# Lists of the experts' tokens: sums of marks by TensorE in place of scatter and gather through DRAM, masks and marks on GpSimd

## The chip, the cores and the metric

The kernel runs on one core of a Trainium2 chip. The metric is the device time of one execution in microseconds (us). The engines of the core are TensorE (PE in the profile), VectorE (DVE), ScalarE (ACT), GpSimd (POOL) and SyncE (SP), which here only issues DMAs.

## The reference, cut to what matters

One decoder layer on x of 16 sequences x 256 tokens x 256 channels, in float32. It has three parts, each with a residual:

```
x = x + ssm(layernorm(x))                     # a scan over the tokens, 16 states per channel
x = x + align(ctx, layernorm(x))              # DTW: rows of ctx summed where the best path goes
x = x + moe(layernorm(x))                     # 64 experts, the best 2 of each token

logits = x_n @ gate                           # 4096 tokens x 64 experts
weights, selected = top_k(logits, 2);  weights = softmax(weights)
y[t] = sum over i of weights[t, i] * (silu(x_n[t] @ w0[e]) * (x_n[t] @ w1[e])) @ wo[e],  e = selected[t, i]
```

So 8192 entries (token, first or second choice) are to be put into 64 lists, one for each expert, and every expert then works on the rows of its list.

## The kernel before, in words

The stages follow each other as blocks, each with its own instruction streams, and a barrier between them: `states` (the scan), the DTW wave and the trace back, `expand`, `experts`, `combine`.

**`states`** begins with eight loads of x, 512 tokens each (`load_x`, L286). DVE takes the statistics of a group in `mean(p)` (L493), which waits for the semaphore of that one load.

**`expand`** (L1529 on) goes over the 16 sequences b in beats. For each b the work is: ACT makes `apart`, the squared distance of each row to the middle of a token's stretch on the path (`far`, L1929); DVE compares it with `reach` and writes the 0/1 masks `on` (`masks`, L1721, two instructions of 128x256); PE multiplies masks by ctx and adds x (`expanded`, L1984: four matmuls with masks, two with the identity, each of 128x256); ACT copies the sum to x (`added`, L1960, line L1962 in the profile); DVE takes mean and variance and a Newton step; ACT normalizes to `xn` (which SP writes to DRAM); PE transposes it (`turn`), ACT copies it (`take_turned`, L1954), PE forms the logits (`logits`, L2005), DVE finds the eight largest and their places (`largest`, `where`), writes `hot`, the 0/1 marks of the two chosen experts (`mark`, L1782), and their sum `chosen` (`choose`, L1789). PE then counts with two matmuls how many earlier entries an expert has (`rank`, L2015), DVE picks an entry's own place (`pick`, `position`) and `address` (L1815) makes of expert and place a line number `slot`. The beats are skewed: in beat b PE works on `rank(b-3)`, `logits(b-2)`, `expanded(b+1)`, `turn(b-1)`, in this order, and DVE in beat b begins with `masks(b+1)` and later has `statistics(b)`, `largest(b-2)` to `choose(b-2)` and `position(b-3)`, `address(b-3)`.

The lists are made in DRAM: `enter(b)` (L1643) on GpSimd issues, for each tile of 128 tokens and each choice, one indirect DMA that writes 128 numbers of 4 bytes into `bucket` (64 in all). After the last beat, the experts are sorted by their counts (`key`, `above`, `my_rank`, `at_rank`, `order`: short steps to and fro between PE and DVE, L1860 to L1879 and L2036 to L2050), SP loads the weights of the first expert as soon as `order` is there, and GpSimd waits until all 64 scatters have landed and gathers from `bucket` the first 256 entries of each expert in the sorted order (L1684, `entries_i`). PE transposes them to `choice`; DVE makes `table`, the row of x_n for each entry (L1923); GpSimd gathers the rows of the first expert (L1691), and the block ends.

**`experts`** (L2072 on) runs 63 ranks, with a static room for each, and then a loop of late tiles for what is left (one pass here). PE goes by ranks; SP loads the weights of rank k when rank k-4 is done (a ring of 4); GpSimd gathers rows four ranks ahead (`gather`) and scatters the results to `outs` (`scatter`). For a late tile SP reads its entries from `bucket` and loads its expert's weights once PE has signalled that rank 59 is done (`done`, given in rank 60). `combine` adds the two results of each token.

The order of the work is written out by hand: the loops in each engine's block say which step stands before which. In `expand` it is for PE

```
for b in range(B + 3):
    if real(b - 3): rank(b - 3)
    if real(b - 2): logits(b - 2)
    if real(b + 1): expanded(b + 1)
    if real(b - 1): turn(b - 1)
```

and on GpSimd `for b in range(B): enter(b)`.

Of the kernel before, what the change touches and what calls it, by code (L numbers as in the profile page):

```python
# [5 lines left out]
ALU = mybir.AluOpType  # L6
# [8 lines left out]
P = 128  # L15
# [152 lines left out]
def states(K):  # L168
# [7 lines left out]
    with ExitStack() as c:  # L176
# [61 lines left out]
        x_in = [sem(f"x_in{g}") for g in range(NP)]  # L238
# [46 lines left out]
        def _(sp):  # L285

            def load_x(p):
                sp.dma_start(K.x[:, p * PTT:(p + 1) * PTT, :],
                             K.x_dram[p * PT:(p + 1) * PT, :].rearrange("(t p) d -> p t d", p=P)).then_inc(x_in[p], 16)
# [199 lines left out]
        def _(dve):  # L489
# [3 lines left out]
            def mean(p):  # L493
                dve.wait_ge(x_in[p], 16)
# [812 lines left out]
def trace_back(K):  # L1307
# [6 lines left out]
    with ExitStack() as c:  # L1314
# [50 lines left out]
        def _(pool):  # L1365
# [15 lines left out]
            pool.wait_ge(set_up, 10)  # L1381
# [147 lines left out]
def expand(K):  # L1529
# [3 lines left out]
    TABS, COUNTED, RANKED, ORDERED, PLACED, LATE_FROM, LATE_OF, TURNED = range(1, 9)  # L1533
    ENTERED = 2 * TT * 16
    ABOVE, AT_RANK, ORDER, MORE, SERVES, ENTRIES, TABLE = range(1, 8)
    with ExitStack() as c:
# [21 lines left out]
        col, eps, expert, row, ones, earlier = K.col, K.eps, K.expert, K.row, K.ones, K.earlier  # L1558
        picked = ring(2, "ex_picked", [P, 2, 2, E])
        nth = ring(2, "ex_nth", [P, 2, 2])  # L1560
        slot = sb("ex_slot", [P, TT, 2], I32)
# [7 lines left out]
        line = sb("ro_line", [P, 1])  # L1569
# [7 lines left out]
        above = sb("ro_above", [E, E])  # L1577
        my_rank = sb("ro_my_rank", [E, 1])
        at_rank = sb("ro_at_rank", [E, E])
        of_rank = sb("ro_of_rank", [E, E])  # L1580
        lines = sb("ro_lines", [E, 1], I32)
        entries_i = sb("ro_entries_i", [E, 2 * P], I32)
        entries = sb("ro_entries", [E, 2 * P])
# [16 lines left out]
        l_ps = [ps(f"ex_l{u}", [P, 4, P]) for u in range(2)]  # L1600
# [15 lines left out]
        slot_ok, placed = sem("ex_slot_ok"), sem("ex_placed")  # L1616
# [7 lines left out]
        ALL = 12  # L1624
# [15 lines left out]
        def _(pool):  # L1640
            imprecise = dict(allow_small_or_imprecise_dtypes=True)

            def enter(b):  # L1643
                pool.wait_ge(slot_ok, b + 1)
                for t in range(2 * b, 2 * b + 2):
                    for i in range(2):
# [33 lines left out]
            for b in range(B):  # L1680
                enter(b)
# [804 lines left out]
```

## Time and profile before

| | us |
|---|---|
| three runs, median | 1364.31 |
| three runs, lowest and highest | 1362.76, 1365.70 |
| profiled execution, span from the first to the last instruction | 1362.8 |
| of it, first beats of `expand` to the end of its last copy of x (719.3 to 822.0) | 102.7 |
| of it, from there to the first work of `experts` (822.0 to 862.2) | 40.2 |
| of it, `experts` up to the late tile's first product (862.2 to 1307.6) | 445.4 |
| `combine` (1325.0 to 1362.8) | 37.8 |

| engine | busy us | share of the span |
|---|---|---|
| PE | 1039.0 | 76% |
| DVE | 904.0 | 66% |
| POOL | 649.3 | 48% |
| ACT | 574.8 | 42% |

The shortest of the three runs is as long as the span, so next to nothing lies around the span. The shares are averages over stages with different limits; for one stage a timeline shows on which engine each step waits. In a timeline a row is: start, duration, engine, line, operation, result and operands, shape, number of merged instructions, and in brackets the idle time of the engine before it with what ended it. "remote" there means that the semaphore's event came late, by the profile, with no instruction that ended just then.

### The profile page before, as it was taken

The numbers are of one execution on the slowest core, as the hardware profiler recorded it, in microseconds if no ns is written. First come the engines' busy times: TensorE is split into PE (matmuls) and PEld (weight loads), VectorE is DVE, ScalarE is ACT, GpSimd is POOL, SyncE is SP. The second block draws the span as 40 slices with busy tenths as digits, with TensorE's granted clock in tenths as the row PEclk, the third lists the DMA queues.
The fourth block names the chain that finished last, engine by engine and source line by source line (L and its number), as shares of the span: only waits on it lengthen the run. The fifth ranks groups of instructions, "written<-read, shape, count | busy, mean of one in ns | idle before, by whom it ended". The sixth has DMA issues, their size and how long they took to land. (4 is left out here: it accounts for less than half of the span.)

```text
span 1362.8 us, 20764 instructions
## 1 busy us (share of the span) xinstructions
PE 1039.0 (76%) x6769; PEld 921.1 (68%) x6769; DVE 904.0 (66%) x2041; ACT 574.8 (42%) x1282; POOL 649.3 (48%) x591
## 2 busy tenths in 40 slices
PE   4767878778787775776567764699999999999940
PEld 3656767767676774665215653699999888888840
DVE  6999999999999984887986664233232232323218
ACT  3768787787878653443404441121121212111100
POOL 4887888878788832000003555334434344434310
PEclk8999999999999997555778796799999999999985
DMA  8544646465555622123030111788778788888629
GB/s 238 194 137 134 182 146 188 152 186 166 169 172 157 183 59 57 31 43 51 33 123 32 40 40 32 259 275 268 267 259 268 268 274 272 274 271 269 238 75 348
DMA packets 163531, 232.62 MB, mean 171 GB/s; under 512 B 34380, under 2 KB 87996, under 8 KB 162656
## 3 DMA queue, kind: packets, MB, share of 16 engines
q1 hardware_dynamic: 145808, 207.79, 48.7%
q0 software_dynamic: 11280, 19.06, 4.2%
q10 hardware_dynamic: 6336, 4.44, 1.0%
q8 instruction: 55, 0.90, 0.3%
q14 instruction: 52, 0.43, 0.1%
HBM read 203.08 MB, written 23.95 MB: 167 GB/s over the span
## 5 line engine op out<-in xcount | busy, mean ns | idle before, releaser
L1011 PE MATMUL st_y_ps<-ident,st_hc 128*128 128x128 f32 x2048 | 274.0, 292 | 113.9 <-DVE st_hc L530 113.9
L1011 PEld LDWEIGHTS st_y_ps<-ident,st_hc 128*128 128x128 f32 x2048 | 255.5, 203 | 136.5 <-DVE st_hc L530 135.6
L413 POOL TENSOR_TENSOR st_u<-st_dx,codes 128x1024 f32<-128x1024 f32 x127 | 296.5, 2360 | 40.9 <-DVE st_h L522 31.9
L522 DVE TENSOR_TENSOR_SCAN st_h<-st_da,st_u 128x512 f32<-128x512 f32 x256 | 297.7, 1204 | 0.8 <-ACT st_da L749 0.8
L2203 PE MATMUL mo_h<-mo_xt,w 128*128 128x128 f32 (+17 forms) x2048 | 281.1, 288 | 1.9 <-DVE mo_xt L2300 1.9
L2203 PEld LDWEIGHTS mo_h<-mo_xt,w 128*128 128x128 f32 x2048 | 270.4, 192 | 6.7 <-issue 2.7
L2306 DVE TENSOR_TENSOR mo_inter<-mo_silu,mo_h 128x128 f32<-128x128 f32 (+17 forms) x256 | 75.7, 304 | 281.2 <-ACT mo_silu L2277 217.1
L2144 POOL DMA_INDIRECT outs<-mo_o,choice x95 | 93.7, 986 | 232.6 <-DVE mo_o L2317 219.4
L2277 ACT ACTIVATE mo_silu<-mo_h 128x128 f32<-128x128 f32 (+17 forms) x256 | 71.7, 290 | 311.8 <-PE mo_h L2203 210.9
L749 ACT ACTIVATE st_da<-st_delta,st_a_neg 128x510 f32<-128x510 f32 x256 | 171.7, 685 | 57.2 <-DVE st_h L522 52.8
L530 DVE TENSOR_TENSOR st_hc<-st_h,st_cps 128x1024 f32<-128x1024 f32 x128 | 152.7, 1193 | 0.0
L2137 POOL DMA_INDIRECT mo_xg<-xn,table x93 | 90.4, 972 | 34.5 <-issue 28.1
L1295 PE MATMUL wv_e<-wv_r,wv_shift 128*128 128x1 f32 x274 | 75.9, 348 | 40.5 <-DVE wv_r L1233 39.8
L2217 PE MATMUL mo_ot_ps<-mo_inter,wo 128*128 128x190 f32 (+16 forms) x512 | 88.1, 305 | 17.1 <-DVE mo_inter L2306 14.3
L1295 PEld LDWEIGHTS wv_e<-wv_r,wv_shift 128*128 128x128 f32 x274 | 68.5, 312 | 48.1 <-issue 46.1
L756 ACT ACTIVATE st_cps<-codes 128x512 f32<-128x512 f32 x128 | 76.7, 599 | 46.1 <-DVE st_hc L530 41.1
L1647 POOL DMA_INDIRECT bucket<-ex_row,ex_slot x64 | 62.2, 972 | 60.6 <-DVE ex_slot L1817 43.8
L2217 PEld LDWEIGHTS mo_ot_ps<-mo_inter,wo 128*128 128x128 f32 x512 | 73.3, 190 | 24.2 <-DVE mo_inter L2306 19.8
L2209 PE MATMUL mo_o_ps<-wo,mo_inter 128*128 128x256 f32 x256 | 73.9, 392 | 0.0
L1285 ACT ACTIVATE wv_r<-wv_e,wv_edge_big 128x1 f32<-128x1 f32 x137 | 35.8, 261 | 64.6 <-PE wv_e L1295 64.6
L1367 POOL IOTA tb_vacant<- 128x2048 int32 x1 | 1.9, 1867 | 104.9 <-POOLq L1108 104.9
L1233 DVE TENSOR_TENSOR_SCAN wv_r<-wv_m,wv_r,wave 128x64 f32<-128x64 f32 x136 | 47.8, 352 | 4.8
(359 smaller groups left out, 1416.4 us busy)
## 6 DMA issues: line engine op xcount, KB each, us to landing
codes<-bc SPq DMA_DIRECT2D x256, 256.0 KB, 3.8
w<-in_L_ffn_w_dram SPq DMA_DIRECT2D x128, 512.0 KB
wo<-in_L_ffn_wo_dram SPq DMA_DIRECT2D x64, 512.0 KB
co_got<-outs SPq DMA_DIRECT2D x16, 512.0 KB, 6.0
wave<-dist SPq DMA_DIRECT2D x16, 274.0 KB
x<-in_x_dram SPq DMA_DIRECT2D x8, 512.0 KB, 9.2
st_cx<-in_ctx_dram SPq DMA_DIRECT2D x8, 512.0 KB, 4.1
dist<-st_dd SPq DMA_DIRECT2D x32, 128.0 KB, 3.6
```

Of the source, the lines that this page charges most:

```text
L413: nc.gpsimd.tensor_tensor(u_sb[k % URING][:, :, :], dx[p % 2][:, :, :], over_chunks(b_sb[k % BRING]), ALU.mult).then_inc(u_ok, 1)
L522: nc.vector.tensor_tensor_scan(h_sb[k % HRING][:, dh, :], da_ps[dh][:, :], u_sb[k % URING][:, dh, :], 0.0, ALU.mult, ALU.add).then_inc(h_o ...
L530: nc.vector.tensor_tensor(hc_sb[k % RING][:, :, :], h_sb[k % HRING][:, :, :], over_chunks(c_ps[k % 2][:, :]), ALU.mult).then_inc(hc_ok, 1)
L749: nc.scalar.activation(by_batch(da_ps[dh][:, :]), by_batch(delta[p % 2][:, dh, :]), ACT.Exp, scale=a_neg[:, dh, n:n + 1]).then_inc(da_ok, 1)
L756: nc.scalar.activation(c_ps[k % 2][:, :], c_sb[k % CRING], ACT.Copy).then_inc(c_ok, 1)
L1011: m = nc.tensor.matmul(y_ps[t // 2][:, t % 2, dh * P:(dh + 1) * P], hc_sb[k % RING][:, dh, t * P:(t + 1) * P], K.ident[:, :], start=False, ...
L1295: nc.tensor.matmul(e_ps[t % 4][:, 0:1], K.shift[:, :], r[:, t + 1, SW:SW + 1], start=True, stop=True).then_inc(e_mm, 1)
L2137: nc.gpsimd.indirect_dma_start(xg[k % XR][0:n, a, :], None, K.xn_dram[:, :], bass.IndirectOffsetOnAxis(ap=K.table[0:n, at:at + 1], axis=0) ...
L2144: nc.gpsimd.indirect_dma_start(K.outs_dram[:, :], bass.IndirectOffsetOnAxis(ap=K.choice[0:n, at:at + 1], axis=0), o_sb[k % XR][0:n, a, :], ...
L2203: ins = nc.tensor.matmul(h_ps[m][:, i, 0:n], K.w[r][i][:, c_, m * P:(m + 1) * P], xt[u][:, c_, 0:n], start=(c_ == 0), stop=(c_ == DC - 1))
L2217: ins = nc.tensor.matmul(ot_ps[:, c_, 0:n], K.w[r][2][:, m, c_ * P:(c_ + 1) * P], inter[m][:, 0:n], start=(m == 0 and c_ == 0), stop=(m == ...
L2306: nc.vector.tensor_tensor(inter[m][:, 0:n], silu[m][:, 0:n], h_ps[m][:, 1, 0:n], ALU.mult).then_inc(inter_ok, 1)
```

## The change

- The lists are no longer read back from DRAM. For each beat DVE writes `in_list`, four 128x256 marks of an entry's place (`enlist`, in place of `address`), GpSimd writes `valued`, the marks of its expert times its number in the tile and times the tile's number (`value`), and PE adds up `valued` x `in_list` over all 64 (tile, choice) pairs in one bank (`enlisted`): row = expert and part, column = place. After the sort two matmuls with `at_rank` give `choice` at once.
- `masks` goes from DVE to GpSimd.
- The 64 scatters to `bucket` stay, for the late tiles, but are issued in `experts`: one before each rank's gather (two before the first). `slot` is computed once at the end of `expand`. SP waits for all of them (`K.placed`) before the late loop.
- One PSUM bank is freed for the sum: both `l_ps` now lie in one.
- The semaphores of the eight x loads become two: one for the first, one for the seven others; `mean(p)` for p of 1 and more waits for all seven.

```diff
@@ states
-        x_in = [sem(f"x_in{g}") for g in range(NP)]
+        x_in = [sem("x_in_first"), sem("x_in_rest")]
...
-                dve.wait_ge(x_in[p], 16)
+                dve.wait_ge(x_in[min(p, 1)], 16 * (NP - 1) if p else 16)
@@ expand, GpSimd
-            def enter(b):
-                pool.wait_ge(slot_ok, b + 1)
-                for t in range(2 * b, 2 * b + 2):
-                    for i in range(2):
-                        nc.gpsimd.indirect_dma_start(
-                            K.bucket_dram[:, :], bass.IndirectOffsetOnAxis(ap=slot[:, t, i:i + 1], axis=0),
-                            row[:, t, i:i + 1], None).then_inc(placed, 16)
+            def masks(b):
+                u = b % 2
+                pool.wait_ge(apart_ok, b + 1)
+                if b >= 2:
+                    pool.wait_ge(e_mm, b - 1)
+                for h in range(2):
+                    m = nc.gpsimd.tensor_scalar(on[u][:, h, :], apart[u][:, h, :], reach[:, h, b:b + 1], None,
+                                                ALU.is_le)
+                m.then_inc(mask, 1)
+
+            def value(b):
+                pool.wait_ge(hot_ok, b + 1)
+                if b >= 3:
+                    pool.wait_ge(list_mm, b - 2)
...
+                nc.gpsimd.tensor_tensor(by_part[:, :, :, 0, :], hots, in_tile, ALU.mult)
+                nc.gpsimd.tensor_tensor(by_part[:, :, :, 1, :], hots, tile_no, ALU.mult).then_inc(valued_ok, 1)
...
+            pool.wait_ge(reach_ok, 2)
+            masks(0)
+            masks(1)
             routing_constants()
             for b in range(B):
-                enter(b)
-            pool.wait_ge(row_ok, ORDER)
-            pool.wait_ge(placed, ENTERED)
-            nc.gpsimd.indirect_dma_start(entries_i[:, :], None,
-                                         K.bucket_dram.rearrange("(l j) a -> l (j a)", j=2 * P),
-                                         bass.IndirectOffsetOnAxis(ap=lines[:, :], axis=0)).then_inc(placed, 16)
+                if real(b + 2):
+                    masks(b + 2)
+                value(b)
             pool.wait_ge(row_ok, TABLE)
@@ expand, VectorE
-            def address(b):
+            def enlist(b):
                 need(place_at[b])
...
+                if b >= 3:
+                    dve.wait_ge(list_mm, b - 2)
+                for t in range(2):
+                    for i in range(2):
+                        m = nc.vector.tensor_scalar(in_list[b % 3][:, t, i, :], K.place[:, :],
+                                                    nth[:, 2 * b + t, i:i + 1], None, ALU.is_equal)
+                m.then_inc(in_list_ok, 1)
...
-                if real(b + 1):
-                    masks(b + 1)
...
+            nc.vector.tensor_tensor(listed[:, :], bank(list_ps)[:, 0:L], vacant[:, :], ALU.add).then_inc(row_ok, 1)
...
-            dve.wait_ge(placed, ENTERED + 16)
-            nc.vector.tensor_copy(entries[:, :], entries_i[:, :]).then_inc(row_ok, 1)
@@ expand, TensorE
+            def enlisted(b):
+                pe.wait_ge(in_list_ok, b + 1)
+                pe.wait_ge(valued_ok, b + 1)
+                for t in range(2):
+                    for i in range(2):
+                        m = nc.tensor.matmul(bank(list_ps)[:, 0:L],
+                                             valued[b % 3][:, t, i, :, :].rearrange("p a e -> p (a e)"),
+                                             in_list[b % 3][:, t, i, :], start=(b + t + i == 0),
+                                             stop=(b == B - 1 and t + i == 2))
+                m.then_inc(list_mm, 1)
...
                 if real(b - 1):
                     turn(b - 1)
+                if real(b - 4):
+                    enlisted(b - 4)
...
+            for h in range(2):
+                m = nc.tensor.matmul(bank(xt_ps[1])[:, h * E:(h + 1) * E], listed[:, h * P:(h + 1) * P], at_rank[:, :],
+                                     start=True, stop=True)
@@ experts, SyncE and GpSimd
+            sp.wait_ge(K.placed, 2 * TT * 16)
             n = late_count(sp)
...
             for k in range(RANKS):
+                for n in range(k, 2 * TT, RANKS):
+                    enter(n)
                 if k + XR < RANKS:
                     gather(k + XR)
```

Three places where instructions now stand otherwise. The numbers behind a tile's name are its buffers. First GpSimd in `expand`, at its constants and the first sequence's four scatters, before (`ex_slot` is the line number, `ex_row` the entry):

```order
L1674 IOTA ro_at 64x64
L1676 MEMSET late_of 128x66
L1677 MEMSET late_at 128x66
L1647 DMA bucket<-ex_row,ex_slot 278528x1 [waits ex_slot_ok]
L1647 DMA bucket<-ex_row,ex_slot 278528x1 x3
```

and now, behind the same constants (`ex_on` are the masks, `ex_valued` the marks with numbers, `ex_hot` DVE's marks of the chosen experts):

```order
L1702 MEMSET late_at 128x66
L1654 TENSOR_SCALAR ex_on0<-ex_apart0,ex_reach 128x256 [waits ex_e_mm,ex_apart_ok]
L1654 TENSOR_SCALAR ex_on0<-ex_apart0,ex_reach 128x256
L1666 TENSOR_TENSOR ex_valued0<-ex_hot0,ex_in_tile 128x4x64 [waits ex_hot_ok]
L1667 TENSOR_TENSOR ex_valued0<-ex_hot0,ex_tile_no 128x4x64
L1654 TENSOR_SCALAR ex_on1<-ex_apart1,ex_reach 128x256 [waits ex_e_mm,ex_apart_ok]
L1654 TENSOR_SCALAR ex_on1<-ex_apart1,ex_reach 128x256
L1666 TENSOR_TENSOR ex_valued1<-ex_hot1,ex_in_tile 128x4x64 [waits ex_hot_ok]
L1667 TENSOR_TENSOR ex_valued1<-ex_hot1,ex_tile_no 128x4x64
```

The four scatters of a beat are gone, and the masks of sequence 3 (the second `ex_on1` pair that is shown) stand behind the marks of sequence 0. Next TensorE in the beat that has logits of sequence 0 and masks of sequence 3 (`ex_l` logits, `ex_e` the sum that becomes x); before:

```order
L2011 MATMUL ex_l0<-gate,ex_xt0 128x64 [waits ex_xt_ok]
L2011 MATMUL ex_l0<-gate,ex_xt0 128x64 x3
L1990 MATMUL ex_e1<-codes,ex_on1 128x256 [waits ex_x_ok,ex_mask]
L1990 MATMUL ex_e1<-codes,ex_on1 128x256
L1992 MATMUL ex_e1<-x,ident 128x256
```

and now, two beats on, with the sums of the lists (`ex_list`) behind the transposes:

```order
L2035 MATMUL ex_l<-gate,ex_xt0 128x64 [waits ex_top,ex_xt_ok]
L2035 MATMUL ex_l<-gate,ex_xt0 128x64 x3
L2014 MATMUL ex_e1<-codes,ex_on1 128x256 [waits ex_x_ok,ex_mask]
L2014 MATMUL ex_e1<-codes,ex_on1 128x256
L2016 MATMUL ex_e1<-x,ident 128x256
L2014 MATMUL ex_e1<-codes,ex_on1 128x256 x2
L2016 MATMUL ex_e1<-x,ident 128x256
L2025 MATMUL ex_xt_ps1<-ident,ex_xn3 128x128 [waits ex_xt_ok,ex_xn_ok]
L2025 MATMUL ex_xt_ps1<-ident,ex_xn3 128x128 x3
L2053 MATMUL ex_list<-ex_in_list0,ex_valued0 128x256 [waits ex_valued_ok,ex_in_list_ok]
L2053 MATMUL ex_list<-ex_in_list0,ex_valued0 128x256 x3
```

The order of logits and `ex_e` is as it was; four matmuls are added behind the transposes. Last SyncE at the end of `experts`, before:

```order
L2069 DMA wo_2<-in_L0_ffn_wo_dram 128x4x256
L2109 TENSOR_LOAD late_n
...
L2121 TENSOR_LOAD late_at
...
L2122 TENSOR_LOAD late_of
...
L2125 DMA mo_to_next<-bucket 128x1
```

and now (branches and register steps between are left out in both):

```order
L2104 DMA wo_2<-in_L0_ffn_wo_dram 128x4x256
L2144 TENSOR_LOAD late_n [waits placed]
...
L2157 TENSOR_LOAD late_at
...
L2158 TENSOR_LOAD late_of
...
L2161 DMA mo_to_next<-bucket 128x1
L2104 ISA [waits mo_done]
L2104 DMA w0_3<-in_L0_ffn_w0_dram 128x2x512
```

Before the late tile's three register loads and its weights there is now a wait for all scatters, the last of which stands on GpSimd behind the results of rank 61.

## Rows read from the trace of the kernel before

**Rows 1.** Busy times by stretch of time, `experts`: PE, PEld, DVE, ACT, POOL, PEclk, DMA share, GB/s.

```profile
862.20:1307.60 445.40, 425.40 (x3096) 401.52 (x3097) 136.14 (x412) 85.63 (x285) 184.36 (x189) 0.99 0.80 265
```

**Rows 2.** Timeline of PE in one undisturbed beat of `expand`.

```profile
738.57 1.08 PE L1990 MATMUL ex_e<-codes,ex_on 128*128 128x256 f32 x4
...
740.78 0.59 PE L1992 MATMUL ex_e<-x,ident 128*128 128x256 f32 x2
```

**Rows 3.** Timeline of ACT in `expand`: copies of x for sequences 2, 4, 5, 15.

```profile
731.56 0.60 ACT L1962 ACTIVATE x<-ex_e 128x512 f32<-128x512 f32 x1 [1.31 <-PE ex_e L1992]
...
741.41 0.60 ACT L1962 ACTIVATE x<-ex_e 128x512 f32<-128x512 f32 x1 [1.89 <-issue]
...
750.59 0.60 ACT L1962 ACTIVATE x<-ex_e 128x512 f32<-128x512 f32 x1 [6.14 <-remote]
...
822.02 0.60 ACT L1962 ACTIVATE x<-ex_e 128x512 f32<-128x512 f32 x1 [6.01 <-PE ex_e L1992]
```

**Rows 4.** Timeline of DVE in `expand`: masks, a beat's first part, logits to marks.

```profile
736.20 0.61 DVE L1727 TENSOR_SCALAR ex_on<-ex_apart,ex_reach 128x256 f32<-128x256 f32 x2
...
751.22 0.75 DVE L1734 BATCH_NORM_STATS2 ex_stats<-x 128x6 f32<-128x256 f32 x2 [4.30 <-ACT x L1962]
...
752.79 0.16 DVE L1817 SCALAR_TENSOR_TENSOR ex_slot<-ex_most_at,ex_nth 128x4 int32<-128x4 uint32 x1
...
824.30 0.36 DVE L1774 MAX8 ex_most<-ex_l 128x8 f32<-128x64 f32 x2
...
825.69 0.22 DVE L1791 TENSOR_TENSOR ex_chosen<-ex_hot 128x128 bf16<-128x128 bf16 x1
```

**Rows 5.** Groups by line, GpSimd, whole span: count, busy us, mean ns of one.

```profile
L413 POOL TENSOR_TENSOR st_u<-st_dx,codes 128x1024 f32<-128x1024 f32 x127 | 296.5, 2360 | 40.9 <-DVE st_h L522 31.9 <-DVE st_u L597 8.6 <-POOL st_dx L401 0.2
...
L1186 POOL TENSOR_SCALAR tb_exit<-ident 128x128 f16<-128x128 f32 x1 | 0.6, 589 | 0.1
```

**Rows 6.** After a pause of PE: busy times 751 to 756, then PE's timeline.

```profile
751.00:756.00 5.00, 4.27 (x14) 3.82 (x15) 3.96 (x24) 2.63 (x7) 2.16 (x3) 0.50 0.16 53
...
816.67 2.02 PE L1990 MATMUL ex_e<-codes,ex_on 128*128 128x256 f32 x4
```

**Rows 7.** Timeline of DVE and PE from the last beat to the first expert.

```profile
840.99 0.15 DVE L1870 COPY ro_my_rank<-ex_e 64x1 f32<-64x1 f32 x1 [3.56 <-remote]
...
847.29 0.15 DVE L1876 CAST ro_lines<-ex_xt_ps 64x1 int32<-64x1 f32 x1 [5.67 <-remote]
...
853.27 0.21 DVE L1923 TENSOR_SCALAR table<-choice 128x96 int32<-128x96 int32 x1
...
841.78 0.69 PE L2048 MATMUL ex_xt_ps<-ro_at_rank,ro_by_number 64*128 64x64 f32 x2
...
862.23 0.97 PE L2189 MATMUL mo_xt_ps<-ident,mo_xg 128*128 128x128 f32 x4 [9.48 <-PEq L1536]
```

**Rows 8.** The last two loads of x (issue, landing), and DVE and ACT behind.

```profile
L288 SPq DMA_DIRECT2D x<-in_x_dram x2: 1705/1774/1843, 5.6 to 7.5; - x2
...
DMA to landing us min/median/max: 10.1/10.3/10.5
...
13.03 1.40 DVE L498 BATCH_NORM_STATS2 st_stats<-x 128x6 f32<-128x256 f32 x4
...
17.55 1.49 ACT L722 ACTIVATE codes<-st_w,st_b_dt 128x512 f32<-128x512 f32 x2 [0.85 <-PE st_w L937]
```

**Rows 9.** End of `experts`: SP, POOL, PE; GB/s in 1.25 us slices from 1280.

```profile
1291.93 0.89 SPq L2069 DMA_DIRECT2D w<-in_L_ffn_w_dram  x2
...
1299.65 0.98 POOL L2144 DMA_INDIRECT outs<-mo_o,choice  x1 [1.61 <-DVE mo_o L2317]
...
1317.02 0.18 POOL L2174 COPY mo_to<-mo_to_next 128x1 int32<-128x1 int32 x1 [1.55 <-DMA outs<-mo_o,mo_to]
...
1307.61 3.83 PE L2203 MATMUL mo_h<-mo_xt,w 128*128 128x128 f32 x32 [1.08 <-DVE mo_xt L2300]
...
GB/s 148 20 241 411 360 329 115 105 0 0 105 356 388 358 155 21 23 82 0 0 0 0 105 5 79 33 0 0 75 30 0 0 0 0 0 0 33 180 393 400
```

More of the change, by code:

```diff
@@ L1568, in expand @@
         by_number = sb("ro_by_number", [P, P])
-        line = sb("ro_line", [P, 1])
+        part = sb("ro_part", [P, 1])
+        dump = sb("ro_dump", [P, L])
+        held = sb("ro_held", [P, 1])
+        vacant = sb("ro_vacant", [P, L])
+        listed = sb("ro_listed", [P, L])
         base = sb("ro_base", [P, 1])
@@ L1599, in expand @@
         xt_ps = [ps(f"ex_xt_ps{u}", [P, DC, L]) for u in range(2)]
-        l_ps = [ps(f"ex_l{u}", [P, 4, P]) for u in range(2)]
+        l_ps = ps("ex_l", [P, 4, P])
+        list_ps = ps("ex_list", [P, 2, D])
         rank_ps = [ps(f"ex_rank{u}", [P, 4, P]) for u in range(2)]
@@ L1718, in _ @@
             nc.vector.tensor_tensor(reach[:, :, :], reach[:, :, :], none[:, :, :], ALU.add).then_inc(reach_ok, 1)
-            dve.wait_ge(reach_ok, 2)
-            def masks(b):
-                u = b % 2
-                dve.wait_ge(apart_ok, b + 1)
-                if b >= 2:
-                    dve.wait_ge(e_mm, b - 1)
-                for h in range(2):
-                    m = nc.vector.tensor_scalar(on[u][:, h, :], apart[u][:, h, :], reach[:, h, b:b + 1], None,
-                                                ALU.is_le)
-                m.then_inc(mask, 1)
             def statistics(b):
@@ L1773, in largest @@
                 for t in range(2):
-                    at_most[b] = did(nc.vector.max(most[:, 2 * b + t, :], l_ps[b % 2][:, t, 0:E]))
+                    at_most[b] = did(nc.vector.max(most[:, 2 * b + t, :], l_ps[:, b % 2 * 2 + t, 0:E]))
             def where(b):
@@ L1837, in _ @@
                 if real(b - 3):
-                    address(b - 3)
+                    enlist(b - 3)
                 if real(b - 2):
@@ L1879, in _ @@
             nc.vector.tensor_copy(K.order[:, :], order_ps).then_inc(row_ok, 1)
+            dve.wait_ge(row_mm, TURNED)
+            did(nc.vector.tensor_copy(K.choice[:, 0:2 * WIDE].rearrange("p (r h) -> p r h", h=2),
+                                      choice_ps[:, 0:WIDE, :]))
+            k = did(nc.vector.tensor_copy(K.choice[:, 2 * WIDE:MT], choice_ps[:, WIDE:E, 0]))
+            need(k)
+            nc.vector.tensor_scalar(K.table[:, :], K.choice[:, :], 1, TOK - 1, ALU.arith_shift_right,
+                                    ALU.bitwise_and).then_inc(row_ok, 1)
             dve.wait_ge(act_ok, 2)
@@ L2443, in build @@
         K.row = sb("ex_row", [P, TT, 2], I32)
+        K.place = sb("ex_place", [P, L], BF16)
+        K.in_tile = sb("ex_in_tile", [P, 2], BF16)
+        K.tile_no = sb("ex_tile_no", [P, TT], BF16)
         run(K, trace_back)
```

129 lines of the change are left out of this document (71 added, 58 removed).

## The prediction

> **What bounds the kernel now.** I read the busy times by stretch first, then the timelines of `expand` engine by engine, then the ends of the two stages beside it. In `experts` PE is busy 425 of 445 us at a granted clock of 0.99 and GpSimd 184 [rows 1]: PE sets the pace and GpSimd has room. `expand` goes otherwise. In undisturbed beats a copy of x follows the last at (741.41 - 731.56) / 2 = 4.93 us, a loop between PE and ACT; DVE's work of a beat just fits in. But from the copy for sequence 2 to that for sequence 15 there are 13 beats in 822.02 - 731.56 = 90.5 us, 6.96 each: the copy at 750.59 comes 9.2 us after the last, and its 6.14 us of idle end with "remote" [rows 3]. Four such pauses stand in the stage, all while GpSimd issues scatters one upon the other; I take them to go with the scatters, which the trace makes likely and does not prove. After the last beat two short hand-overs from PE to DVE hang in the same way: DVE idles 3.56 and 5.67 us, the second 4.8 us past the end of PE's matmuls at 842.47 [rows 7].
>
> **The beat of `expand`.** This decides. On GpSimd the masks of sequence b+3 now stand behind the marks of sequence b, and those need DVE's marks, which need PE's logits of b. On PE, the logits of b are the last thing ahead of the sum that waits for the masks of b+3. So a loop closes that wasn't there: logits, DVE, marks, masks, sum, copy, next logits. Before, DVE made these masks at its leisure, ahead of the statistics. I count from the start of one copy of x.
>
> - To DVE's statistics 751.22 - 750.59 = 0.63; from there to the address step 752.79 - 751.22 = 1.57 [rows 3, 4]: 2.2.
> - In place of the address step four comparisons of 128x256. DVE's masks, 4-byte, are 0.61 a pair [rows 4], so up to 1.2; with 2-byte operands I take the half, 0.6 (bounds 0.2 and 1.2): 2.8. The logits are out before that, so PE's part in them is covered.
> - From the largest to the end of `chosen` 825.69 + 0.22 - 824.30 = 1.6 [rows 4]: 4.4.
> - Two products of 256 numbers on GpSimd. 1024 take 2.36 us [rows 5], a quarter 0.59, and something fixed: 0.7 each (0.5 to 1.0): 5.8.
> - Two masks on GpSimd. None of this shape is in the trace: not under DVE's 0.30 each [rows 4]; a 128x128 one took 0.589 [rows 5], twice that is 1.18. I take 0.5, nearer the lower, since the other also changes the type: 6.8. Four semaphores on the way, 0.05 each: 7.0.
> - The sum: 740.78 + 0.59 - 738.57 = 2.8 at full clock [rows 2]: **9.8**.
>
> In this beat PE has nothing to do from the end of the logits, at about 2.2, to 7.0. Before, such pauses of 4 to 5 us were each followed by matmuls at the lower level: in 751 to 756 the granted clock was 0.50, that is 1.2 GHz, and four matmuls of the sum took 2.02 in place of 1.08 [rows 2, 6]. Wholly at that level the sum is 2.8 x 2.02 / 1.08 = 5.2 and the beat 12.2; as now and then part of it will run at 2.4 GHz, I take **12.0** (9.8 to 12.2, wider with GpSimd's bounds). The list's four matmuls stand where PE waits for ACT's copy of the transposes, and cost nothing as long as the beat is set by DVE and GpSimd. The first two masks need no marks, so up to the copy at 731.56 I leave all as it is. Then 13 x 12.0 = 156.0 in place of 90.5: **+65.5**.
>
> The Trainium skill (GPSIMD Engine Reference, section 4.1, Engine selection) speaks against this edit: element-wise work belongs on VectorE and is about two times slower on GpSimd for two inputs, while one input is about line rate. If both masks took twice DVE's 0.61 a pair, they would be 1.2 in place of 1.0, the beat 12.2, and the whole 2.6 us more than the sum below; no row here shows this comparison on GpSimd.
>
> **The end of `expand`.** The two hangs go with the scatters: about 2.5 (3.56 less a us of matmuls) and 4.8 [rows 7]. The gather from DRAM goes: from DVE's first read of the sort's result at 847.29 to the end of `table` at 853.48 there were 6.2 us, mostly waiting for it; now two copies and the shift come straight behind the order, 1.5 with two more matmuls on PE. That is -4.7. Added are the sum of the list's last beat and two DVE steps of 128x256, beside PE's ranking for the most part: +1.0 (0 to 2). From the table to PE's first work, 862.23 - 853.48 = 8.75, nothing changes: the same two gathers, barrier and weights. **-11.0** (-8 to -13).
>
> **The first stage.** DVE's statistics of the second group of x began at 13.03; now they wait for all eight loads, of which the last was issued at 7.5 and took 10.1: 17.6 [rows 8]. DVE needs 1.4 and about 0.4 for them, then ACT takes a root and a reciprocal, about 0.5, ahead of `codes`, which so starts at 19.95, not 17.55 [rows 8]. Its 0.85 of idle there was PE's, and is covered. The scans follow `codes` without a gap: **+2.4** (0 if a later wait takes it up, 2.6 at most).
>
> **`experts`.** 64 scatters of 0.96 and 0.3 to the next are 81 us more for GpSimd, 184 + 81 of 445 [rows 1]; gathers are four ranks ahead, so none of it is waited for: 0. But the late tile's weights now stand behind the last scatter. That is issued behind the results of rank 61, 1299.65 + 0.98 + 0.3 [rows 9], takes 0.96, and lands perhaps 1.55 later, as the result did that ends in GpSimd's idle of 1.55 [rows 9]: 1303.4. Then SP does three register loads and a small DMA that before were long done, for which I take 2 (0.5 to 4; no row shows them alone): 1305.4. Issued at 1291.93 the weights were in at about 1298.5, the end of the high slices, 6.6 later [rows 9]; so now at 1312, where PE wanted them at 1307.61 [rows 9]. **+5** (2 to 7).
>
> **The sum.** 65.5 - 11.0 + 2.4 + 5 = +61.9. The profiled execution had a span of 1362.8, the median of the three runs is 1364.3; on the median that is **1426**.
>
> **Rivals.**
>
> - *The loop stays open* (faster). If masks came early enough, the beat would be the 4.93 of [rows 3], without pauses: 13 x 4.93 = 64.1, -26.4, and in all -30: 1334. It decides at a beat of 7.2, where 13 beats and the other terms cancel. For it speaks that masks have three beats in which they could be made; against it that GpSimd goes in order, and that even with GpSimd at no cost the loop is 9.8 - 2.4 = 7.4.
> - *The clock stays up.* Short beats leave PE little pause, beat 9.8: 127.4, +36.9, in all +33: 1398. Against it, the drop in [rows 6] after pauses as long.
> - *GpSimd is dearer.* Marks 1.0 and masks 1.18 each, +2.0 a beat: 14.0, +91.5, in all +88: 1452. The Trainium skill (GPSIMD Engine Reference, section 1, Specifications) names a cause: GpSimd shares its SBUF interfaces with VectorE and contends with VectorE instructions of two SBUF inputs. The 2360 ns mean in [rows 5], beside a busy DVE, shows no such thing by itself.
> - *The pauses move along.* With 64 scatters in `experts` the "remote" waits, some 24 us in all with the two at the end, come there, where PE sets the pace: 1450 with the beat of 12.0. Against it, GpSimd's runs of DMAs are shorter there, since it waits for results in between.
>
> **How the numbers follow.** Forecast 0.55; clock up 0.17; GpSimd dear 0.14; pauses move along 0.08; loop open 0.06. The range 1395 to 1455 takes in the bounds of the terms and all cases but the open loop and the far ends of the two slowest. About 0.2% is what a measurement of this kernel can tell from no change; every case but the open loop is slower by more, and only a beat near 7.2 would fall within: faster 0.06, same 0.01, slower 0.93.
>
> **What would show it.** Copies of x (`added`) about 12 us apart from sequence 3 on, with no "remote" before them; each sum of PE waiting for GpSimd's `ex_on`, GpSimd's `ex_valued` for DVE's `ex_chosen`; PEclk in these slices well under 0.87; `table` about 1.5 us behind `order`; the second statistics of the first stage at 17.6; PE waiting some 5 us before the late tile's first product. A beat near 5 would make the whole prediction wrong; one near 10 at full clock, its size.

## The result, and the profile after

The changed kernel takes 1552.4 us (median of four runs, 1549.6 to 1554.8) where the kernel before takes 1364.4: 1.138 times as long, 95% interval 1.136 to 1.139. The forecast was 1426, range 1395 to 1455. The direction was right, the size was not: +188, not +62. The profiled execution has a span of 1551.4. It divides so:

| stretch | forecast | before | after | difference |
|---|---|---|---|---|
| to PE's first work of `expand` | +2.4 | 719.36 | 720.76 | +1.40 |
| from there to the copy of x for sequence 2 | 0 | 12.20 | 15.31 | +3.11 |
| 13 beats, to the copy for sequence 15 | +65.5 | 90.46 | 167.91 | +77.45 |
| to PE's first work of `experts` | -11.0 | 40.21 | 28.66 | -11.55 |
| static ranks, to the last transposing back (`mo_o_ps<-ident,mo_ot`) | 0 | 442.69 | 556.12 | **+113.43** |
| late tile, to `combine` | +5 | 20.13 | 24.94 | +4.81 |
| `combine` | 0 | 37.75 | 37.70 | -0.05 |
| sum | +61.9 | 1362.8 | 1551.4 | +188.6 |

The end of `expand` came as forecast, the late tile in its total; the beats came 12 us dearer, the start of `expand` 3. One term, put down as nothing, is 60% of all that happened. First the stage where the forecast held, ACT's copies of x; they answer to [rows 3]:

```profile
736.07 0.60 ACT L1986 ACTIVATE x<-ex_e 128x512 f32<-128x512 f32 x1 [1.07 <-PE ex_e L2016]
748.03 0.60 ACT L1986 ACTIVATE x<-ex_e 128x512 f32<-128x512 f32 x1 [8.93 <-PE ex_e L2016]
...
774.22 0.60 ACT L1986 ACTIVATE x<-ex_e 128x512 f32<-128x512 f32 x1 [10.23 <-PE ex_e L2016]
787.48 0.60 ACT L1986 ACTIVATE x<-ex_e 128x512 f32<-128x512 f32 x1 [10.22 <-PE ex_e L2016]
...
903.98 0.60 ACT L1986 ACTIVATE x<-ex_e 128x512 f32<-128x512 f32 x1 [11.02 <-PE ex_e L2016]
```

No copy waits for "remote" any more; each waits some 10 us for PE's sum. The average beat is 167.91 / 13 = 12.92 us. The beat from 774.22 on, in DVE's, GpSimd's and PE's timelines, shows the loop step by step:

```profile
778.59 0.23 DVE L1808 TENSOR_TENSOR ex_chosen<-ex_hot 128x128 bf16<-128x128 bf16 x1
...
778.90 0.61 POOL L1666 TENSOR_TENSOR ex_valued<-ex_hot,ex_in_tile 128x256 bf16<-128x256 bf16 x1 [10.26 <-DVE ex_chosen L1808]
779.47 0.64 POOL L1667 TENSOR_TENSOR ex_valued<-ex_hot,ex_tile_no 128x256 bf16<-128x256 bf16 x1
780.09 1.81 POOL L1654 TENSOR_SCALAR ex_on<-ex_apart,ex_reach 128x256 f32<-128x256 f32 x2
...
781.96 2.07 PE L2014 MATMUL ex_e<-codes,ex_on 128*128 128x256 f32 x4 [5.49 <-POOL ex_on L1654]
...
786.38 1.06 PE L2016 MATMUL ex_e<-x,ident 128*128 128x256 f32 x2
```

From the copy to the end of `ex_chosen` 4.6 us, marks to 780.1, masks to 781.9, sum to 787.4. Busy times by stretch show the level of PE's clock in that sum: 0.62, then 0.50, which is 1.2 GHz, as [rows 6] had it after a pause (columns as in [rows 1]).

```profile
780.00:784.00 4.00, 2.04 (x5) 1.69 (x6) 0.15 (x1) 0.00 (x0) 1.90 (x3) 0.62 0.00 0
784.00:787.48 3.48, 3.48 (x11) 2.65 (x10) 0.00 (x0) 0.00 (x0) 0.00 (x0) 0.50 0.00 0
```

Three more places, each a line: `codes` of the first stage, against 17.55 in [rows 8]; `table`, whose end is 1.6 us behind DVE's first read of the sort's result at 923.14, against 6.2 in [rows 7]; and the late tile's first product, which waits 7.5 us for its weights, against 1.08 for DVE in [rows 9].

```profile
19.98 1.25 ACT L722 ACTIVATE codes<-st_w,st_b_dt 128x512 f32<-128x512 f32 x2
...
924.55 0.21 DVE L1910 TENSOR_SCALAR table<-choice 128x96 int32<-128x96 int32 x1
...
1497.96 5.34 PE L2247 MATMUL mo_h<-mo_xt,w 128*128 128x128 f32 x32 [7.49 <-DMA wo<-in_L_ffn_wo_dram]
```

Now the stage where it failed. Busy times of the static ranks, to be read against [rows 1], which reach 2.7 us further, to the late tile: PE is busy some 50 us longer, at a granted clock of 0.91 in place of 0.99, and idle some 62 us more.

```profile
932.60:1488.70 556.10, 474.04 (x3090) 442.25 (x3090) 136.38 (x408) 87.74 (x285) 245.93 (x252) 0.91 0.64 209
```

What it waited for stands in the waits of that stretch (who waited, for whom, us in total, times, longest). In the kernel before, ACT's activation waited for "remote" twice in all of `experts`:

```profile
ACT mo_silu L2277 <- remote: 4.4, 2, 2.5
...
PE mo_ot_ps L2217 <- DVE mo_inter L2306: 14.3, 21, 1.3
```

and now:

```profile
ACT mo_silu L2321 <- remote: 99.6, 43, 4.7
...
PE mo_ot_ps L2261 <- DVE mo_inter L2350: 47.1, 34, 3.9
```

So signals from PE to ACT come late, ACT and DVE run late behind it, and PE waits for DVE's products. One pair of ranks in the timelines of GpSimd, ACT and PE shows when:

```profile
1100.72 1.00 POOL L2180 DMA_INDIRECT outs<-mo_o,choice  x1 [8.00 <-DVE mo_o L2361]
1102.03 0.92 POOL L2180 DMA_INDIRECT outs<-mo_o,choice  x1 [0.30 <-issue]
1103.25 0.99 POOL L2186 DMA_INDIRECT bucket<-ex_row,slot  x1 [0.30 <-issue]
1104.55 0.98 POOL L2173 DMA_INDIRECT mo_xg<-xn,table  x1 [0.31 <-issue]
1105.84 0.98 POOL L2180 DMA_INDIRECT outs<-mo_o,choice  x1 [0.31 <-issue]
1107.12 0.97 POOL L2186 DMA_INDIRECT bucket<-ex_row,slot  x1 [0.30 <-issue]
1108.39 0.99 POOL L2173 DMA_INDIRECT mo_xg<-xn,table  x1 [0.30 <-issue]
1109.69 0.88 POOL L2173 DMA_INDIRECT mo_xg<-xn,table  x1 [0.30 <-issue]
```

```profile
1104.92 0.31 ACT L2321 ACTIVATE mo_silu<-mo_h 128x166 f32<-128x166 f32 x1 [2.81 <-PE mo_h L2247]
1107.88 0.31 ACT L2321 ACTIVATE mo_silu<-mo_h 128x166 f32<-128x166 f32 x1 [2.64 <-PE mo_h L2247]
1111.43 0.31 ACT L2321 ACTIVATE mo_silu<-mo_h 128x166 f32<-128x166 f32 x1 [3.25 <-remote]
1112.28 0.31 ACT L2321 ACTIVATE mo_silu<-mo_h 128x166 f32<-128x166 f32 x1 [0.54 <-remote]
```

```profile
1103.60 3.54 PE L2247 MATMUL mo_h<-mo_xt,w 128*128 128x166 f32 x24
...
1107.54 1.29 PE L2247 MATMUL mo_h<-mo_xt,w 128*128 128x166 f32 x8
```

GpSimd (first fence) issues eight indirect DMAs without a pause, two of them the new scatters; before there were six. PE (last fence) had the first three products by 1107.1 and the fourth by 1108.8 (these ends are modelled, but the fourth product had begun at 1107.54). But ACT's third activation runs at 1111.43, 0.9 us after GpSimd's run has ended, and the fourth behind it.

The kernel before has the same hold-up in a milder form, and its profile seldom calls it "remote". These are the first and last DMA of a run of six there, PE's first three products and ACT's third and fourth activation:

```profile
1105.24 1.02 POOL L2144 DMA_INDIRECT outs<-mo_o,choice  x1 [6.59 <-DVE mo_o L2317]
...
1111.64 0.93 POOL L2137 DMA_INDIRECT mo_xg<-xn,table  x1 [0.30 <-issue]
...
1108.10 3.18 PE L2203 MATMUL mo_h<-mo_xt,w 128*128 128x148 f32 x24
...
1113.81 0.48 ACT L2277 ACTIVATE mo_silu<-mo_h 128x148 f32<-128x148 f32 x2 [1.89 <-PE mo_h L2203]
```

The third product ended at 1111.28 and was taken up 2.5 us later, 1.2 us behind the run; over the 29 runs of six of that trace the median is 2.35 us. PE had other work in the meantime and then idled only 0.98 us. So two DMAs more did not bring the hold-up in; they made it longer than PE's other work.

### The profile page after: what moved, and what is told of

Its sections match the earlier page's. It is cut to its first block and busy times, and to the rows that moved or that the text cites. A ratio compares the mean times of both kernels' runs of the same rounds, so it can differ in the third digit from the quotient of the medians.

```text
span 1551.4 us, 21033 instructions
## 1 busy us (share of the span) xinstructions
PE 1128.3 (73%) x6833; PEld 991.3 (64%) x6833; DVE 918.0 (59%) x2059; ACT 577.5 (37%) x1282; POOL 697.8 (45%) x661
## 5 line engine op out<-in xcount | busy, mean ns | idle before, releaser
L2247 PE MATMUL mo_h<-mo_xt,w 128*128 128x128 f32 (+17 forms) x2048 | 308.7, 307 | 8.6 <-DMA wo<-in_L_ffn_wo_dram 7.5
L2247 PEld LDWEIGHTS mo_h<-mo_xt,w 128*128 128x128 f32 x2048 | 299.8, 211 | 13.7 <-issue 9.6
L2261 PE MATMUL mo_ot_ps<-mo_inter,wo 128*128 128x190 f32 (+16 forms) x512 | 109.0, 345 | 80.4 <-DVE mo_inter L2350 47.1
L2261 PEld LDWEIGHTS mo_ot_ps<-mo_inter,wo 128*128 128x128 f32 x512 | 84.6, 215 | 95.5 <-DVE mo_inter L2350 56.3
L2014 PE MATMUL ex_e<-codes,ex_on 128*128 128x256 f32 x128 | 58.0, 602 | 72.0 <-POOL ex_on L1654 72.0
L2014 PEld LDWEIGHTS ex_e<-codes,ex_on 128*128 128x128 f32 x128 | 37.6, 308 | 82.9 <-POOL ex_on L1654 75.1
L1748 DVE BATCH_NORM_STATS2 ex_stats<-x 128x6 f32<-128x256 f32 x32 | 12.0, 418 | 108.1 <-ACT x L1986 108.1
L1666 POOL TENSOR_TENSOR ex_valued<-ex_hot,ex_in_tile 128x256 bf16<-128x256 bf16 x16 | 9.8, 614 | 142.7 <-DVE ex_chosen L1808 142.7
```

Source lines behind the costliest of these rows:

```text
L2014: nc.tensor.matmul(e_ps[b % 2][:, j, :], on[b % 2][:, h, j * P:(j + 1) * P], K.cx[:, 2 * b + h, :], start=(h == 0), stop=False)
L2247: ins = nc.tensor.matmul(h_ps[m][:, i, 0:n], K.w[r][i][:, c_, m * P:(m + 1) * P], xt[u][:, c_, 0:n], start=(c_ == 0), stop=(c_ == DC - 1))
L2261: ins = nc.tensor.matmul(ot_ps[:, c_, 0:n], K.w[r][2][:, m, c_ * P:(c_ + 1) * P], inter[m][:, 0:n], start=(m == 0 and c_ == 0), stop=(m == ...
```

## The experiments

Ten runs, in three steps. The first separated the two large costs.

**e1: no scatters in `experts`.**

```diff
-            sp.wait_ge(K.placed, 2 * TT * 16)
...
-                for n in range(k, 2 * TT, RANKS):
-                    enter(n)
```

> The changed kernel with the 64 scatters to bucket left out of experts, and the wait for them ahead of the late tile with them (bucket keeps its first filling; with this input the one late pass reads nothing of it that is used). Theory A (each scatter holds up the signals of PE, so that PE, ACT and DVE wait for each other): the static ranks go from 556 us back to about 443, and the late tile's wait of 7.5 us to about 1; in all 1552 - 113 - 5 = 1434 us. Theory B (the scatters are innocent; the pauses in experts come from something else that the change moved, such as the tiles' places in memory or late weights): only the wait goes, about 1547. Theory C (GpSimd falls behind because its queue is longer): also about 1434, but then the idle of PE in the changed kernel would have ended on gathers, which it doesn't; it ends on DVE's products.

Measured 1433.7 us. The static ranks take 441.3 us and the clock is back:

```profile
930.20:1371.50 441.30, 423.38 (x3091) 400.09 (x3091) 134.82 (x408) 85.60 (x285) 183.90 (x188) 0.99 0.80 267
```

The late tile's wait is 1.3 us. Theory A holds, B falls: the 64 scatters cost 115 us there, which this forecast had as nothing. Theory C gives the same time; against it stands that of PE's waits in the changed kernel only the first, of 3.7 us, ends on a gather.

**e2: masks ahead of marks.**

```diff
+            masks(2)
             for b in range(B):
-                if real(b + 2):
-                    masks(b + 2)
+                if real(b + 3):
+                    masks(b + 3)
                 value(b)
```

> The changed kernel with GpSimd's order in expand turned round: masks of sequence b+3 ahead of the marks of sequence b. Theory A (the serial loop logits - marks - masks - sum sets the beat of 12.9 us): the loop is open, the beat falls to the 4.9 of the undisturbed loop between PE and ACT, 13 beats take 64 in place of 168 us, the kernel 1552 - 104 = 1448. Theory B (GpSimd's work itself is the limit: 3.1 us of masks and marks a beat, and what it costs DVE by contention): a beat of 6 to 8, 1460 to 1490. Theory C (the clock stays low and the sums at 1.2 GHz set it): a beat of 6 to 7, with the granted clock near 0.5, 1465 to 1475. The static ranks of experts stay at 556.

Measured 1449.5 us. From the copy for sequence 2 to that for sequence 15:

```profile
735.32 0.60 ACT L1987 ACTIVATE x<-ex_e 128x512 f32<-128x512 f32 x1 [1.08 <-PE ex_e L2017]
...
804.27 0.60 ACT L1987 ACTIVATE x<-ex_e 128x512 f32<-128x512 f32 x1 [3.12 <-PE ex_e L2017]
```

That is 68.95 us, 5.30 a beat in place of 12.92, at a full clock. Theory A holds: the order of two steps on GpSimd had closed the loop. The 0.4 over 4.93 is most likely DVE's, which is busy 15.27 of the 16.1 us from 761.5 on:

```profile
761.50:777.60 16.10, 14.89 (x93) 12.71 (x92) 15.27 (x79) 9.11 (x21) 9.11 (x13) 1.00 0.14 50
```

**e3: the same scatters with rows of 64 bytes.**

```diff
-                nc.gpsimd.indirect_dma_start(K.bucket_dram[:, :],
+                nc.gpsimd.indirect_dma_start(K.lines_dram[:, :],
                                              bass.IndirectOffsetOnAxis(ap=K.slot[:, t, i:i + 1], axis=0),
-                                             K.row[:, t, i:i + 1], None).then_inc(K.placed, 16)
+                                             K.x[:, t, 16 * i:16 * i + 16], None).then_inc(K.placed, 16)
```

> The changed kernel with the same 64 scatters to the same line numbers, each writing 128 rows of 64 bytes of x into a tensor of its own instead of 128 numbers of 4 bytes into bucket (with this input the late pass uses nothing of bucket). Theory A1 (the hold-ups come from writing single 4-byte numbers, several of one stretch of 64 bytes): they vanish, static ranks about 443 to 450, the kernel about 1440. Theory A2 (they come from the number of small writes or of indirect DMAs, whatever the width): as the changed kernel, static ranks 550 to 560, 1545 to 1555.

Measured 1548.1 us, static ranks 552.3. A1 falls as far as 64 bytes go.

**e4: the kernel before, scatters kept back to the end of the beats.**

```diff
+            pool.wait_ge(slot_ok, B)
             for b in range(B):
                 enter(b)
```

> The kernel before with its 64 scatters kept back until the last sequence's line numbers are there, so that no scatter runs beside the beats. Theory A (the pauses that end with remote go with the scatters): from the copy of x for sequence 2 to that for sequence 15 there are 64 us, not 90.5; then the scatters take 64 x 1.28 = 82 us on their own from about 812 to 894, and the kernel is about 1364 + 45 = 1409. Theory B (the pauses come from something else in the beat): still 90 us, and the kernel about 1364 + 70 = 1434.

Measured 1408.3 us. The copies for sequences 2 and 15 now stand 64.0 us apart, 4.92 a beat, and none waits for "remote":

```profile
731.98 0.60 ACT L1963 ACTIVATE x<-ex_e 128x512 f32<-128x512 f32 x1 [1.31 <-PE ex_e L1993]
...
796.00 0.60 ACT L1963 ACTIVATE x<-ex_e 128x512 f32<-128x512 f32 x1 [2.69 <-PE ex_e L1993]
```

So the pauses of [rows 3] do go with the scatters, as the prediction took them to.

The second step asked what about a scatter holds PE's signals up: that it is small, that it is one more, or that it makes GpSimd's run longer.

**e5: the same number of scatters with rows of 1 KB**, like the scatters of results.

```diff
-                nc.gpsimd.indirect_dma_start(K.bucket_dram[:, :],
-                                             bass.IndirectOffsetOnAxis(ap=K.slot[:, t, i:i + 1], axis=0),
-                                             K.row[:, t, i:i + 1], None).then_inc(K.placed, 16)
+                nc.gpsimd.indirect_dma_start(K.lines_dram[:, :],
+                                             bass.IndirectOffsetOnAxis(ap=K.row[:, t, i:i + 1], axis=0),
+                                             K.x[:, t, :], None).then_inc(K.placed, 16)
```

> The changed kernel with each of the 64 scatters writing 128 rows of 1 KB of x into a tensor of its own, at the places in the order of the rows, in place of 128 numbers of 4 bytes into bucket (with this input the late pass uses nothing of bucket). These are the size and kind of the scatters of results that the kernel makes anyway. Theory A1 (small writes hold up the signals): static ranks 443 to 455 us, the kernel about 1440 to 1450. Theory A2 (what counts is that GpSimd issues eight indirect DMAs one upon the other in each pair of ranks in place of six, whatever they move): static ranks 540 to 570, the kernel 1540 to 1565.

Measured 1550.3 us, static ranks 555.4, 46 waits of ACT for "remote" with 103 us. What the scatters move makes no difference.

**e6: the same scatters in GpSimd's pause.**

```diff
-                for n in range(k, 2 * TT, RANKS):
-                    enter(n)
...
+                if k % 2 == 0:
+                    pool.wait_ge(inter_ok, (k + 1) * FC)
+                    enter(k)
+                    enter(k + 1)
                 scatter(k)
```

> The changed kernel with the same 64 scatters, of 4 bytes a row, to the same lines, but no longer in one row with the gathers and the scatters of results: two of them per pair of ranks, in the pause that GpSimd has there, behind a wait for the last product of the wide rank. GpSimd then has runs of six and of two. Theory A2 (the length of a run of indirect DMAs without a pause decides): the hold-ups go, static ranks 443 to 460, the kernel 1440 to 1457. Theory A3 (each added scatter costs its 1.8 us wherever it stands): static ranks about 556, the kernel about 1552. The late tile's wait stays in both.

Measured 1453.8 us, static ranks 456.1. GpSimd's timeline now has a run of six, a pause, and a run of two:

```profile
1117.38 0.97 POOL L2180 DMA_INDIRECT outs<-mo_o,choice  x1 [3.33 <-issue]
...
1123.72 0.90 POOL L2173 DMA_INDIRECT mo_xg<-xn,table  x1 [0.31 <-issue]
1126.88 1.01 POOL L2186 DMA_INDIRECT bucket<-ex_row,slot  x1 [2.26 <-DVE mo_inter L2352]
1128.19 0.98 POOL L2186 DMA_INDIRECT bucket<-ex_row,slot  x1 [0.30 <-issue]
1131.20 0.97 POOL L2180 DMA_INDIRECT outs<-mo_o,choice  x1 [2.03 <-DVE mo_o L2363]
```

The same 64 scatters cost 15 us over e1 in place of 115, and ACT's waits for "remote" are 3.5 us in all:

```profile
ACT mo_silu L2323 <- remote: 3.5, 3, 1.2
```

A2 holds: the length of a run decides, not the scatter. A3 falls.

**e9: runs of seven and one**, made from e6 by moving one of the two scatters back into the run.

```diff
+                if k % 2:
+                    enter(k)
+                if k + 1 == RANKS:
+                    enter(k + 1)
                 if k + XR < RANKS:
                     gather(k + XR)
...
                 if k % 2 == 0:
                     pool.wait_ge(inter_ok, (k + 1) * FC)
                     enter(k)
-                    enter(k + 1)
```

> The changed kernel with one of the two scatters per pair of ranks left in the run (seven indirect DMAs one upon the other in place of eight) and the other one in GpSimd's pause as in e6. In e6 (six and two) the static ranks took 456 us, in the changed kernel (eight) 556. Theory A2a (signals are held from about the sixth DMA of a run to its end): one DMA less is 1.3 us less of the 3.1 us held per pair, static ranks 490 to 520. Theory A2b (a limit that is reached at the eighth): static ranks 450 to 465. Theory A3 (each scatter in the run costs 1.8 us): 500 to 510; it fell with e6 for a scatter outside the run.

Measured 1498.4 us, static ranks 501.3, "remote" in between:

```profile
ACT mo_silu L2326 <- remote: 38.5, 22, 3.2
```

So there is no step at the eighth, as theory A2a has it. (A3 forecast the same time, but had fallen with e6.) Over the 441.3 of e1 (six) the seventh DMA, with the other one in the pause, costs 60 us, 1.9 per pair of ranks; the eighth some 55 more.

The third step put together what had been learned.

**e7: masks first, scatters behind a branch, three semaphores for x.** The branch is taken when more than one late pass is needed; only such a pass reads `bucket`. `masks` as in e2, and:

```diff
                 if k + XR == RANKS:
+                    with pool.If(late_count(pool) > 1):
+                        for n in range(2 * TT):
+                            enter(n)
+                        pool.wait_ge(K.placed, 2 * TT * 16)
...
-        x_in = [sem("x_in_first"), sem("x_in_rest")]
+        x_in = [sem("x_in_first"), sem("x_in_second"), sem("x_in_rest")]
```

> The changed kernel with masks ahead of marks on GpSimd, the 64 scatters only behind a branch that is taken when more than the one late pass is needed (not with this input), no wait for them on SyncE, and three semaphores for the loads of x (first, second, the other six), so that the second statistics wait for one load as before. If the three costs are independent: 1552.4 - 102.9 (masks first) - 118.7 (no scatters) - 2.4 = 1328 us, 0.973 of the kernel before. If opening the loop and taking the scatters away meet in some stage (the end of expand, a lower clock): 1330 to 1345. If the statistics of the second group aren't on the path: 1331.

Measured 1335.3 us, 0.978 of the kernel before (0.977 to 0.979): it is faster than both kernels. Static ranks 441.3, 13 beats 68.99, end of `expand` 28.96, and `codes` starts at 17.54 again:

```profile
17.54 0.69 ACT L722 ACTIVATE codes<-st_w,st_b_dt 128x512 f32<-128x512 f32 x1 [0.85 <-PE st_w L937]
...
832.00:1273.30 441.30, 423.58 (x3091) 400.05 (x3091) 134.72 (x408) 85.55 (x285) 183.39 (x188) 0.99 0.80 267
```

The 7 us over the sum of the three are no new wait: against the changed kernel's trace the static ranks, the beats and the late tile give -114.8, -98.9 and -2.8, as in e1 and e2, and the start -2.1; that makes 1333, its span. The sum had counted too much: e1's profiled execution was 2.6 us shorter ahead of `expand`'s third copy, where it has the same code (PE's first sums ran at 2.4 GHz there, at 1.2 in the changed kernel's and e7's), and e2's 0.8 there and 3.9 in the static ranks, which e7 can't lose twice. An input that takes the branch was not tried; it would pay for 64 scatters in one run.

**e8: e7 with the masks on DVE again**, where they stood before (the function moved as it is, `gpsimd` to `vector`).

> The version e7 with the masks back on DVE, at the place where they stood before; GpSimd keeps the marks. What moving the masks to GpSimd is worth, once it doesn't close a loop. In e2 DVE sets the beat of 5.3 us (15.27 of 16.1 us busy). Theory A (DVE is the bound): two masks add 0.61 to each beat, 5.3 to 5.9 us, 13 beats 77 in place of 69, less the 3 us that the first four masks take longer on GpSimd at the start of expand: 1335 + 8 - 3 = 1340. Theory B (GpSimd and DVE hold each other up, so that taking masks from GpSimd makes DVE faster): beat 4.9 to 5.3, 1327 to 1332. Other stages as in e7.

Measured 1335.3 us, the same as e7 to 0.1, between the two expectations. But the stretches differ. 13 beats take 71.62 in place of 68.99, and the end of `expand` 30.70 in place of 28.96. Back come 2.8 us ahead of the copy for sequence 2 (12.37 from PE's first work in place of 15.17) and 2.4 behind the static ranks, where both kernels have the same code. Most of what comes back is the clock: e10, with e7's code in `expand`, takes 13.03 for that start with PE's first sums at 2.4 GHz, and the late tile's 32 matmuls of `mo_h` took 5.46 us in e7 and 3.83 in e8. So the equal times are in part chance; at an equal clock the masks on GpSimd would be worth some 4 us, by an estimate from these rows that no run shows.

**e10: e7 without the branch**, all 64 scatters made, spaced as in e6, and SP waits for them behind the late weights.

```diff
+                sp.wait_ge(done, g + 1)
+                settle(sp)
+                load_weights(K, sp, e, RANKS % WRING)
                 sp.wait_ge(indices, g * 2 + 1)
+                sp.wait_ge(K.placed, 2 * TT * 16)
                 settle(sp)
                 sp.dma_start(to_next[:, :], K.bucket_dram[bass.ds(at, P), :]).then_inc(to_in, 16)
-                sp.wait_ge(done, g + 1)
-                settle(sp)
-                load_weights(K, sp, e, RANKS % WRING)
```

> The version e7 without its branch: all 64 scatters are made whatever the input, two per pair of ranks in GpSimd's pause as in e6, and SyncE waits for them only behind the late weights, ahead of the read of bucket. Theory A2: e7 plus what e6 had left over e1 in the static ranks (456.1 - 441.3 = 14.8 us): 1335 + 15 = 1350, the late tile's first product 3 to 4 us behind the last static one, not 12.7. Rival (the wait for the scatters holds up DVE's index, and the late tile with it): 1354 to 1357.

Measured 1343.9 us, 0.985 of the kernel before (0.984 to 0.986). Static ranks 452.6, the late product 5.5 us behind the last static one, nearer to the 3 to 4 of theory A2 than to the 12.7 of e6. It is 9 us slower than e7, not 15: the scatters cost 11.3 in the static ranks, and 2.1 came back in PE's first sums, which ran at 2.4 GHz in this execution. It makes the scatters with any input.

## Why the prediction was wrong

**The step that failed** is the first sentence on `experts`: 64 scatters "are 81 us more for GpSimd", gathers are four ranks ahead, "so none of it is waited for: 0". GpSimd indeed had the room (busy 245.9 of 556) and no gather came late. But the cost of a scatter there is not GpSimd's time. It is that a run of indirect DMAs without a pause holds PE's signals up, and two scatters made each pair's run eight long in place of six, more than PE had other work for: +113.4 (e1, e6, e9).

The mechanism stood among the rivals, *the pauses move along*, with a chance of 0.08 and a price of 24 us. Both were wrong by the same shortcut. The price took the pauses of `expand` as a sum that moves. What [rows 3] show is a price per run: a copy 9.2 us after the last in place of 4.93, so 4.3, and GpSimd's run there is one of eight (739.15 to 749.26). `experts` has 32 pairs of ranks, nearly each of which would become a run of eight: 32 x 4.3 = 136 us. Measured are 113.4 / 32 = 3.5 per pair. And the argument against it, that runs are shorter there since GpSimd waits for results in between, was never counted: a look at GpSimd's timeline would have given six per pair, and six and two make eight. With that price the sum would have been 61.9 + 136 = +198; measured +188.6. Such a fit would have been partly luck: beats behind a pause are longer too, and if all 26.4 us of the four pauses are counted, the price is 6.6 per run and the term 211. Either price says that the term is not nothing.

**The beat** was right in its mechanism (e2), and low in one term: masks on GpSimd 0.5 each, measured 0.92, which is 0.8 of the 0.9 us by which 12.92 stands over 12.0. From the copy to the end of `ex_chosen` it took 4.6 (forecast 4.4), the marks 1.2 (1.4), the sum at 1.2 GHz 5.5 (5.2). Only in some beats did part of it run at 2.4 GHz, as in the one of 11.96 from 736.07 on.

**"Up to the copy at 731.56 I leave all as it is"** missed 3.1 us. Of these 0.8 are PE's wait for GpSimd's first two masks: e1, e5, e6 and e10, where PE waits for the same two masks, take 13.0 for this stretch, where the kernel before took 12.20. The other 2.3 are the clock: PE's first four matmuls with masks took 2.08 us here and 1.13 in those four runs. Why the level differs between executions of the same code is not known.

**The end of `expand`** (-11.0, measured -11.55) and **the first stage** (`codes` at 19.95, measured 19.98) came as worked out, each by following one wait to its end. Of the last, 1.4 us are left where `expand` starts.

**The late tile** (+5, measured +4.81) had its wait right and its size by luck. The first product begins 9.2 us behind the last transposing back in place of 2.7, so 6.5 later, not 4.4, and at the lower clock takes 1.5 longer; but from GpSimd's last copy to `combine` 4.8 us pass in place of 8.0. Without scatters and wait (e1) the stretches behind the static ranks are only 2.6 us shorter than with them. Why the way to `combine` became shorter is not known.

*The loop stays open* and *the clock stays up* did not happen; e2 shows what the first would have been. *GpSimd is dearer* was right in part: masks were, marks not.

## What to carry to other kernels

Moving indirect DMAs to a stage where the issuing engine is half idle is not free: count how many it then issues without a pause, and if the trace shows steps that start late behind such runs anywhere, called "remote" or not, price them per run and multiply by the runs of the new place. Here six in a row already held signals up, but PE had other work for that time; eight cost 3.5 us per pair of ranks, and the two added DMAs put into a pause 0.5. And when a step moves to an engine that works in order, ask what it now stands behind and whether that needs its own result: two lines exchanged were worth 103 us.

## What the runs showed of the hardware

- While GpSimd issues indirect DMAs without a pause, signals from PE to ACT begin to come late within the run; in 28 of the 30 runs of eight, ACT's last activation that waited for "remote" starts 1.0 to 1.7 us behind the run's end. With runs of six the third product was taken up 2.35 us late (median, kernel before). The waits called "remote" grow with the length: 3.5 us in all of `experts` for runs of six and two, 38.5 for seven and one, 99.6 for eight. Rows of 4 bytes, 64 bytes and 1 KB give the same (556, 552, 555 us). In the pair shown, DVE took up ACT's product at once (1107.88 + 0.31, and DVE started at 1108.22), so there it was PE's signals that were late. Why a run holds them up is not known from these runs.
- GpSimd's marks hold DVE up. DVE's `ex_nmr`, a step of 128x2, took a median of 161 ns in the kernel before and 607 ns now, when it starts beside `ex_valued` of 0.61 us:

```profile
L1768 DVE SCALAR_TENSOR_TENSOR ex_nmr<-ex_mv,ex_rstd x16: 160/161/161, 727.9 to 826.0; 128x2 f32<-128x2 f32 x16
```

```profile
L1782 DVE SCALAR_TENSOR_TENSOR ex_nmr<-ex_mv,ex_rstd x16: 160/607/609, 732.7 to 908.7; 128x2 f32<-128x2 f32 x16
```

  The first is of the kernel before, the second of the changed one (minimum, median, maximum ns). The Trainium skill (GPSIMD Engine Reference, section 1, Specifications) says that GpSimd shares its SBUF interfaces with VectorE and contends with VectorE instructions of two SBUF inputs. The trace agrees: `ex_nmr` is one of these. Not every GpSimd instruction did this: beside a mask, at 732.71, it took 0.16.
- Two masks, each one tensor compared with a number per partition, took 1.81 us on GpSimd and 0.61 on DVE [rows 4]: three times, where the Trainium skill (GPSIMD Engine Reference, section 4.1, Engine selection) has about line rate for one input. The measurement decides.
